# Graph network block on one Trainium2 core: edge rows joined by ScalarE in the first stage, attention logits made by VectorE alone, spare count cells zeroed first

## The reference

```python
# L0: three attention layers, 4 heads of 24
h = x @ W; e = leaky_relu(alpha_s[src] + alpha_d[dst], 0.2)
alpha = softmax of e over the edges of each dst
x = relu(segment_sum(h[src] * alpha, dst) + b)
# L1: sum of neighbours, two dense layers, norm over the nodes
# L2: dot-product attention over the edges, scores clipped to +-10
# L3: messages from edge features
msg = relu(x[src] + edge_attr @ We + be); aggr = segment_sum(msg, dst)
# then two dense layers and a norm over the nodes
```

## Time and profile before

| | us |
|---|---|
| median of 3 runs (5859.54 to 5867.38) | 5861.98 |
| profiled execution | 5863.81 |
| its span | 5862.1 |

### The profile page before, as it was taken

The page is one execution under the profiler, slowest core; times in us unless marked ns, Lnnn a source line. Parts: engine busy times, 40 slices in busy tenths (PEclk is TensorE's granted clock), DMA queues, the critical chain, the costliest instruction groups (busy, mean ns, idle before and its releaser), DMA issues. The chain is left out here.

```text
span 5862.1 us, 68109 instructions
## 1 busy us (share of the span) xinstructions
PE 3511.6 (60%) x25247; PEld 2219.0 (38%) x25248; DVE 3123.5 (53%) x3383; ACT 2625.6 (45%) x4143; POOL 3883.7 (66%) x3309
## 2 busy tenths in 40 slices
PE   3211222221034699988999889997868781667764
PEld 2211111111034455555555555554433330455542
DVE  3644555554369555445555455555579992333323
ACT  1000000000023689888888789894059891222211
POOL 1888888888884577666776578773020787777772
PEclk7555555555566899999999999998989995677765
DMA  8222222222279699757997479875542332332222
GB/s 296 20 18 20 20 18 10 1 1 0 9 251 361 169 195 199 161 115 150 195 193 156 103 164 201 184 153 152 178 166 79 109 130 74 110 81 74 75 53 24
DMA packets 427191, 683.75 MB, mean 117 GB/s; under 512 B 177678, under 2 KB 272397, under 8 KB 422768
## 3 DMA queue, kind: packets, MB, share of 16 engines
q0 software_dynamic: 236096, 287.22, 31.9%
q1 hardware_dynamic: 172432, 350.48, 17.8%
q10 hardware_dynamic: 18336, 41.70, 2.1%
HBM read 540.73 MB, written 138.43 MB: 116 GB/s over the span
## 5 line engine op out<-in xcount | busy, mean ns | idle before, releaser
L330 POOL DMA_INDIRECT counts<-plcell_add,plcell_slot x806 | 1253.9, 1556 | 385.4 <-issue 223.2
L1704 POOL DMA_INDIRECT emxg<-xtab,emsrc x856 | 944.0, 1103 | 448.4 <-issue 257.8
L714 ACT ACT_TABLE_LOAD x1 | 1.3, 1283 | 1613.2 <-PE mtps L702 1613.2
L377 PE MATMUL plpsR<-plpiece,plbefore 128*128 128x500 bf16 (+1 forms) x81 | 47.1, 582 | 813.8 <-DVE plranked L507 800.6
L422 DVE TENSOR_REDUCE plnlow<-plsame 128x13 f32<-128x1664 bf16 x62 | 117.0, 1888 | 661.6 <-DMA counts<-plcell_add,plcell_slot 661.5
L1788 PE MATMUL dotbanks<-emmsg,emsame 128*128 128x96 f32 x1712 | 316.3, 344 | 237.4 <-DVE emsame L1968 230.1
L1176 ACT ACTIVATE ga1prob<-ga1psE,ga1src_fifth 128x512 f32<-128x512 f32 (+1 forms) x700 | 407.2, 680 | 81.8 <-PE ga1psE L1281 79.1
L1176 ACT ACTIVATE ga2prob<-ga2psE,ga2src_fifth 128x512 f32<-128x512 f32 (+1 forms) x700 | 407.5, 683 | 77.0 <-PE ga2psE L1281 74.1
L1176 ACT ACTIVATE ga0prob<-ga0psE,ga0src_fifth 128x512 f32<-128x512 f32 (+1 forms) x700 | 407.1, 678 | 77.7 <-PE ga0psE L1281 74.7
L1788 PEld LDWEIGHTS dotbanks<-emmsg,emsame 128*128 128x128 f32 x1712 | 287.2, 250 | 382.2 <-issue 379.5
L1281 PE MATMUL ga0psE<-ident,ga0logit 128*128 128x128 f32 x2500 | 394.5, 288 | 55.8 <-DMA ga0logit<-log_counts 32.7
(11 more groups left out here) (403 smaller groups left out, 8577.9 us busy)
## 6 DMA issues: line engine op xcount, KB each, us to landing
ga0logit<-log_counts POOLq DMA_DIRECT2D x88, 512.0 KB
ga1logit<-log_counts POOLq DMA_DIRECT2D x88, 512.0 KB
ga2logit<-log_counts POOLq DMA_DIRECT2D x88, 512.0 KB
counts<-plzeros SPq DMA_DIRECT2D x32, 1250.0 KB, 32.7
mthalf<-counts SPq DMA_DIRECT2D x50, 800.0 KB
log_counts<-mtlogs SPq DMA_DIRECT2D x25, 1600.0 KB
ginhalf<-counts SPq DMA_DIRECT2D x50, 800.0 KB
dotlogs<-log_counts ACTq DMA_DIRECT2D x25, 1600.0 KB
```

What stands on the lines that cost most here:

```text
L330: nc.gpsimd.indirect_dma_start(counts[w][:, :], bass.IndirectOffsetOnAxis(ap=cell_slot[:, g % 2, j:j + 1], axis=0), cell_add[:, g % 2, j:j ...
L377: nc.tensor.matmul(psR[:, f // RANK_BANK, 0:k * BINS], before[:], piece[:, n % 2, f:f + k, :].rearrange("p t b -> p (t b)"), start=True, s ...
L714: nc.scalar.activation(logs[:, n % OUTS, q, :], ps[:, u % 3, 0:BW], ACT.Ln, bias=tiny[:, 0:1], scale=math.e).then_inc(log_made, 1)
L1704: nc.gpsimd.indirect_dma_start(xg[:, h, t, :], None, xtab[:, :], bass.IndirectOffsetOnAxis(ap=src[:, g, t:t + 1], axis=0)).then_inc(gather ...
```

## The change

Three things. (1) The spare cells of both tables are zeroed ahead of the bulk, each by one row of 128 cells from one partition. (2) In the first stage, once the sorted list is cleared, SP loads each group's features, ACT joins them with the ends into whole rows (two copies), and SP stores these in DRAM; this is paced by two adds of table 1 per group. The scatter then loads finished rows into three buffers with one DMA per group, and the slots of a stage with one DMA; its copies, its memset and its loads of ends and features are gone. (3) In the layers DVE makes the kept logits alone: a clamp as for the added tiles, then an addition of the loaded mask; ACT's bias instruction is gone, and the mask buffers are freed by DVE's addition. DVE's order in a run becomes: added clamps, kept clamps, kept additions, then the output or the columns. Semaphores are renamed accordingly.

```diff
+WHOLE_BUFS = 3
...
-        edges = {"slot": nc.dram_tensor("edge_slot", [P, ET], i32), "ends": nc.dram_tensor("edge_ends", [P, ET, 2], f32),
+        edges = {"slot": nc.dram_tensor("edge_slot", [P, ET], i32), "rows": nc.dram_tensor("edge_rows", [P, ET, RW], f32),
...
+        feat = sb("feat", [P, WHOLE_BUFS, G, ED])
+        whole = sb("whole", [P, WHOLE_BUFS, G, RW])
...
                 for part, done in zip(counts, zeroed):
+                    sp.dma_start(part[NP * NP:NP * NP + P, :].rearrange("(p f) o -> p (f o)", p=1), zeros[0:1, 0:P]).then_inc(done, 16)
+                for part, done in zip(counts, zeroed):
                     v = part[0:NP * NP, :].rearrange("(p j f) o -> j p (f o)", p=P, f=ZF)
                     for j in range(ZEROS):
                         sp.dma_start(v[j], zeros[:]).then_inc(done, 16)
-                    sp.dma_start(part[NP * NP:NP * NP + P, :], zeros[:, 0:1]).then_inc(done, 16)
...
+                features = a["edge_attr_32"].rearrange("e k -> (e k)")
+                most = features[0:(P - 1) * ET * ED].rearrange("(p f) -> p f", f=ET * ED)
+                rest = features[(P - 1) * ET * ED:E * ED].rearrange("(p f) -> p f", p=1)
+
+                def load_features(g):
+
+                    k = g % WHOLE_BUFS
+                    if g >= WHOLE_BUFS:
+                        sp.wait_ge(whole_made, 2 * (g - WHOLE_BUFS + 1))
+                    flat = feat[:, k, :, :].rearrange("p t k -> p (t k)")
+                    sp.dma_start(flat[0:P - 1, :], most[:, g * G * ED:(g + 1) * G * ED]).then_inc(feat_loaded[k], 16)
+                    n = min(G, EREST - g * G)
+                    if n > 0:
+                        sp.dma_start(flat[P - 1:P, 0:n * ED], rest[:, g * G * ED:(g * G + n) * ED]).then_inc(feat_loaded[k], 16)
+
+                sp.wait_ge(feat_cleared, 1)
+                load_features(0)
+                for g in range(NG):
+                    sp.wait_ge(added[1], 16 * (4 * SORTED_GROUPS + 2 * g + 1))
+                    if g + 1 < NG:
+                        load_features(g + 1)
+                    sp.wait_ge(whole_made, 2 * g + 2)
+                    sp.dma_start(edges["rows"][:, g * G:(g + 1) * G, :], whole[:, g % WHOLE_BUFS, :, :]).then_inc(whole_stored[g % WHOLE_BUFS], 16)
...
-                sp.dma_start(edges["ends"][:, :, :], ends[:]).then_inc(stored, 16)
                 sp.dma_start(edges["slot"][:, :], block_i[:]).then_inc(stored, 16)
-                sp.wait_ge(stored, 64)
+                sp.wait_ge(stored, 48)
+                for k in range(WHOLE_BUFS):
+                    sp.wait_ge(whole_stored[k], 16 * len(range(k, NG, WHOLE_BUFS)))
...
+                nc.vector.memset(feat[:], 0.0).then_inc(feat_cleared, 1)
...
+            @block.scalar
+            def _(act):
+                act.wait_ge(ends_made, 1)
+                for g in range(NG):
+                    k = g % WHOLE_BUFS
+                    uses = range(k, g + 1, WHOLE_BUFS)
+                    act.wait_ge(feat_loaded[k], sum(32 if n * G < EREST else 16 for n in uses))
+                    if g >= WHOLE_BUFS:
+                        act.wait_ge(whole_stored[k], 16 * (g // WHOLE_BUFS))
+                    nc.scalar.activation(whole[:, k, :, 0:ED], feat[:, k, :, :], ACT.Copy).then_inc(whole_made, 1)
+                    nc.scalar.activation(whole[:, k, :, ED:RW], ends[:, g * G:(g + 1) * G, :], ACT.Copy).then_inc(whole_made, 1)
...
-                    step(nc.vector.tensor_copy(ends[:, :, 0], local_i[:]))
+                    nc.vector.tensor_copy(ends[:, :, 0], local_i[:]).then_inc(ends_made, 1)
+                    dve.wait_ge(ends_made, 1)
...
-    STAGES = 2
+def edge_scatter(nc, ctx, edges, tag, first, last):
+
+
+
+    STAGES = 3
     count = last - first
-    LISTS = 4
-    slot = sb("slot", [P, LISTS, G], i32)
-    ends = sb("ends", [P, LISTS, G, 2])
-    feat = sb("feat", [P, STAGES, G, ED])
-    stage = sb("stage", [P, STAGES, G, RW])
-    feat_cleared, staged = (sem(n) for n in ("feat_cleared", "staged"))
-    list_loaded = [sem(f"list_loaded{k}") for k in range(LISTS)]
-    feat_loaded = [sem(f"feat_loaded{k}") for k in range(STAGES)]
-    scattered = [sem(f"scattered{k}") for k in range(STAGES)]
+    slot = ctx.enter_context(nc.sbuf_tensor(tag + "slot", [P, max(count, 1) * G], i32))
+    stage = ctx.enter_context(nc.sbuf_tensor(tag + "stage", [P, STAGES, G, RW], f32))
+    slots_loaded = nc.alloc_semaphore(tag + "slots_loaded")
+    rows_loaded = [nc.alloc_semaphore(f"{tag}rows_loaded{k}") for k in range(STAGES)]
+    scattered = [nc.alloc_semaphore(f"{tag}scattered{k}") for k in range(STAGES)]

     def steps(pool):
-        nc.gpsimd.memset(feat[:], 0.0).then_inc(feat_cleared, 1)
-        pool.wait_ge(feat_cleared, 1)
-        flat = a["edge_attr_32"].rearrange("e k -> (e k)")
-        most = flat[0:(P - 1) * ET * ED].rearrange("(p f) -> p f", f=ET * ED)
-        rest = flat[(P - 1) * ET * ED:E * ED].rearrange("(p f) -> p f", p=1)
-        loads = lambda i: 32 if (first + i) * G < EREST else 16

         def load(i):

-            g, k, m = first + i, i % STAGES, i % LISTS
-            pool.dma_start(slot[:, m, :], edges["slot"][:, g * G:(g + 1) * G]).then_inc(list_loaded[m], 16)
-            pool.dma_start(ends[:, m, :, :], edges["ends"][:, g * G:(g + 1) * G, :]).then_inc(list_loaded[m], 16)
-            rows = feat[:, k, :, :].rearrange("p t k -> p (t k)")
+            k, g = i % STAGES, first + i
             if i >= STAGES:
-                pool.wait_ge(staged, 2 * (i - STAGES + 1))
-            pool.dma_start(rows[0:P - 1, :], most[:, g * G * ED:(g + 1) * G * ED]).then_inc(feat_loaded[k], 16)
-            n = min(G, EREST - g * G)
-            if n > 0:
-                pool.dma_start(rows[P - 1:P, 0:n * ED], rest[:, g * G * ED:(g * G + n) * ED]).then_inc(feat_loaded[k], 16)
-
+                pool.wait_ge(scattered[k], 16 * G * (i // STAGES))
+            pool.dma_start(stage[:, k, :, :], edges["rows"][:, g * G:(g + 1) * G, :]).then_inc(rows_loaded[k], 16)
+
+        pool.dma_start(slot[:], edges["slot"][:, first * G:last * G]).then_inc(slots_loaded, 16)
         load(0)
+        pool.wait_ge(slots_loaded, 16)
         for i in range(count):
-            k, m = i % STAGES, i % LISTS
+            k = i % STAGES
             if i + 1 < count:
                 load(i + 1)
-            pool.wait_ge(feat_loaded[k], sum(loads(n) for n in range(k, i + 1, STAGES)))
-            pool.wait_ge(list_loaded[m], 32 * (i // LISTS + 1))
-            if i >= STAGES:
-                pool.wait_ge(scattered[k], 16 * G * (i // STAGES))
-            nc.gpsimd.tensor_copy(stage[:, k, :, 0:ED], feat[:, k, :, :]).then_inc(staged, 1)
-            nc.gpsimd.tensor_copy(stage[:, k, :, ED:RW], ends[:, m, :, :]).then_inc(staged, 1)
-            pool.wait_ge(staged, 2 * i + 2)
+            pool.wait_ge(rows_loaded[k], 16 * (i // STAGES + 1))
             for t in range(G):
-                nc.gpsimd.indirect_dma_start(edges["sorted"][:, :], bass.IndirectOffsetOnAxis(ap=slot[:, m, t:t + 1], axis=0),
+                nc.gpsimd.indirect_dma_start(edges["sorted"][:, :], bass.IndirectOffsetOnAxis(ap=slot[:, i * G + t:i * G + t + 1], axis=0),
                                              stage[:, k, t, :], None).then_inc(scattered[k], 16)
                 yield i * G + t
...
-        BIAS_AT = (1, 5)
+        MASK_FREE_AT = (3, 5)
...
-                        wait(sp, act_biased, free)
+                        wait(sp, logit_ready, free)
...
-                def finish_logit(r, q):
+                def clamp_kept(r, q):

                     j, c, h = runs[r]
                     first, width = RUN_FIRST[c] * P, RUN_TILES[c] * P
-                    dve.wait_ge(act_biased, act_count[r] + kept_tiles(j).index(q) + 1)
+                    if r >= L_BUFS:
+                        dve.wait_ge(turned, run_end(r - L_BUFS))
+                    nc.vector.tensor_scalar(logit[:, r % L_BUFS, q, 0:width], src_row[:, h, first:first + width], dst_bias[:, j % 2, q, h:h + 1],
+                                            low_bias[:, j % 2, q, h:h + 1], ALU.add, ALU.max).then_inc(kept_clamped, 1)
+
+                def finish_logit(r, q):
+
+                    j, c, h = runs[r]
+                    width = RUN_TILES[c] * P
+                    k, uses = mask_slot(r, q)
+                    dve.wait_ge(kept_clamped, kept_count[r] + kept_tiles(j).index(q) + 1)
+                    dve.wait_ge(mask_loaded[k], 16 * (uses + 1))
                     part = logit[:, r % L_BUFS, q, 0:width]
-                    nc.vector.scalar_tensor_tensor(part, src_row[:, h, first:first + width], least[:, block_first[j] + q, h:h + 1], part, ALU.max, ALU.add).then_inc(logit_ready, 1)
+                    nc.vector.tensor_tensor(part, part, mask[:, k, 0:width], ALU.add).then_inc(logit_ready, 1)
...
+                        clamp_kept(r, q)
+                    for q in kept_tiles(0):
                         finish_logit(r, q)
...
```

(47 more changed lines are left out.)

5 lines of the change are left out of this document (1 added, 4 removed).

## The result

The changed kernel takes 6017.0 us (median of 6 runs, 6009.5 to 6033.8) against 5862.2 for the kernel before (5855.3 to 5867.4): ratio 1.0266, 95% interval 1.0252 to 1.0281. Forecast were 5752 and a range that ended at 5835.

| stage | before | changed | e1_split |
|---|---|---|---|
| first stage | 1647.2 | 1897.2 | 1642.2 |
| its adds, seventh to last start | 1503.0 | 1776.8 | 1521.4 |
| table stage | 278.6 | 275.9 | 275.4 |
| three layers with their setups | 2112.0 | 2010.6 | 2013.9 |
| all behind them | 1824.3 | 1823.9 | 1821.3 |

The account below looks back on a forecast made before the run. Bounds: GpSimd's late-starting row of count adds in the first stage; ScalarE biases and DMA in the layers. First stage -20 (-26 + 6) and three layers -90 from 5863.8 give 5753.8, against the median 5752; range 5675 to 5835.

Parts of the forecast that it names:

- Spare cells first: Start of first stage: both 14 us zeroing tails go, seventh add starts at 111.5 instead of 137.5; 26 us, bounds 20 to 28.
- Edge rows in the first stage: First stage: joining rows there disturbs the count adds by 0.05 us per transfer, 124 transfers, 6 us; bounds 0 and 27.
- The rival of disturbed adds: First stage: the 124 transfers cost the adds 0.22 us each, 27 us instead of 6; total 5775, chance 0.08.
- Table stage: Table stage: 5 of 62 groups are scattered there, covered by VectorE's work; zero change.
- Scattering in the layers: Attention layers: GpSimd is relieved of 59 us per layer, worth nothing by itself, but pays for VectorE making all logits.
- The ScalarE bias: Attention layers: removing 168 biases saves 0.44 us per half run without top sums, 25 and 29 us per layer.
- VectorE makes all logits: Attention layers: VectorE rises to 462 us; 16 us of three-tile and 14 of four-tile gain remain, 30 per layer.
- The floor of 96 us of DMA work: Four-tile blocks in the layers: 96 of 101.2 us are DMA work, leaving 5 open; 3.5 taken per block.
- The point against: Layers: longer VectorE operations slow GpSimd's scatter issue by 0.08 us, 20 us per layer, inside the 59 relieved.
- the 1.81 from which it decides: Layers: mean GpSimd scatter issue, in us, from which GpSimd being locked out decides the time.
- the third rival: Layers: GpSimd locked out by VectorE, scatter issue rising from 1.22 to 2.07 us; +64 per layer, total 6036, chance 0.06.
- the prediction's own signs of being right: Among others: seventh add near 111, adds 1.86 to 1.9 us apart, three-tile halves 2.5 to 2.7, scatter issue under 1.4.

Follow-up runs that it names:

- e1_split: The changed kernel with each first-stage feature load cut in two, 112 and 15 partitions: 5757.2 us, ratio 0.9833 to the kernel before.
- e4_join_only: e1_split with the layers' logits made as before (ScalarE adds biases), GpSimd still scattering finished rows: 5801.6 us, ratio 0.9896 to the kernel before.
- e3_logits_only: The kernel before with only the layers' logits made by VectorE, GpSimd still joining the rows: 5881.2 us, ratio 1.0040.

## Why the prediction was wrong, point by point

1. *Spare cells first*: right in kind and nearly in size. 26 us forecast, 23.7 measured, inside 20 to 28. The bulk of table 1 is late next, as the prediction said, but not in the way it had put it, with the six adds on table 0 through by 110. The fifth add lands only when the bulk is through: in the changed kernel and the seven runs with the spare cells first it starts anywhere from 103.3 to 108.0, and the sixth always at 111.8 to 112.3, while the rate of the zeroing falls to 0 by 111 (changed kernel). The seventh then follows the sixth, at 113.8 where 111.5 was forecast.
2. *Edge rows in the first stage*: **this step failed**. It priced 124 transfers at 0.05 us, at most 0.22 (27 us); the row of adds grew by 273.8. (The 59 small loads of the last partition, which it names, are not in the 124.) The price came from the clears of the sorted rows, 54 transfers of 272 KB, which landed 2.0 us after their issue (median). I took the feature load for a transfer of the same kind, counting it and its bytes, and never asked how its 127 partitions are shared out. The kernel of before had no such load on the SP queue to warn of it (the same 127 partitions were loaded by GpSimd's queue); but it cuts the loads of src and dst at 112 on the SP queue, which was there to be read. The Trainium skill's rule cited above gives 127 packets on one engine, which I could have had before. The rival of disturbed adds had the right place and 27 us for 274. With the load cut, the step is 18.4 us: three times the 6 taken, inside 0 to 27, 17 of it the loads.
3. *Table stage*: zero forecast, 2.7 us gained.
4. *Scattering in the layers*: wrong as put. "It waits already, so this is worth nothing by itself" was argued from GpSimd's idle time; e4_join_only gives it 50 us. GpSimd's waits for clamps do not mean that its masks come in time: PE stood for masks 76 us in the three layers. "It pays for point 6" was right, and e3_logits_only shows how fully: without the relief point 6 loses.
5. *The ScalarE bias*: 0.44 us per half run, to the hundredth in the half runs shown (3.46 to 3.02, 2.92 to 2.48).
6. *VectorE makes all logits*: the additions 1.258 us, where I took 1.16; VectorE 456 us, forecast 462. The sum of 30 per layer met 31.9, 37.2 and 28.9. Its split did not: in layers 0, 1 and 2 the three blocks of three tiles gave 8.8, 14.5 and 6.3 us for 16, but the four of four tiles 20.9, 20.4 and 20.3 for 14. So the sum came out by two errors that cancel, which is luck. The floor of 96 us of DMA work was none: block 4 of layer 1 (counted from 0) takes 89.9.

*The point against*: VectorE's longer row did slow GpSimd, by more than the 20 us that I allowed: scatters 247 x 0.22 = 55 us and masks 132 x 0.19 = 25 us in layer 1. The mean of 1.44 stayed below the 1.81 from which it decides by the prediction, a bound that counts the relief in. This is the third rival's mechanism at a quarter of its price. Slower it came out, but not by that rival. Two of the prediction's own signs of being right failed: the adds came 2.22 us apart, not 1.86 to 1.9, and the scatter issue took 1.40 to 1.44 us, not under 1.4.

*The forecast of 5752 beside e1_split's 5757.* With the load cut the total nearly meets the forecast, but not by its terms: in the profiled executions the first stage gave 5 us for 20, the layers 98 for 90, the table stage 3 and the parts behind the layers another 3 for nothing.

## What to carry to other kernels

Before moving a transfer to another queue, read its outermost size, not only its bytes: 127, 97 or 61 partitions from the SP queue passed packet behind packet, 112, 126 or 128 did not, and the transfers beside them (here the adds) came late by a share of it. A cut that costs one more issue per group was worth 255 us of the row of adds. And idle time of an engine is no proof that relieving it is worthless: where it sits in a chain with others, try the parts apart and together (-50, +19 and -96 us here, in three layers).

## What the runs showed of the hardware that was not expected

- A transfer of 127 partitions of 1664 B from the SP queue passed packet behind packet, as on one DMA engine, in 9.6 us at some 22 GB/s; cut at 112 the same bytes passed in 2.1 us at up to 365 GB/s. The SP queue's next issue behind it took 2.69 us instead of 0.25; behind 61 or 97 such partitions it took 0.26, and why isn't known.
- The load delayed the count adds by 31 to 36 ns for each packet of 77 ns, from 61 packets to 127, and the slack that the adds had did not absorb it.
- 128 two-byte cells spread over 128 partitions kept each table waiting 14 us behind its bulk; as one row of 256 B ahead of it they let the first add start 1.1 us after the time estimated for the bulk's end (62), at 63.1.
- With VectorE making all logits (busy 462 us of 663 instead of 353 of 665), GpSimd's work beside it took longer: its copies of 128x416 from 0.90 to 1.25 us, its issues of scatters from 1.22 to between 1.36 and 1.44, of mask additions from 1.09 to 1.27. Without that part of the change (e4_join_only, layer 1) the issues took 1.23 and 1.08. The single operation on two SBUF tensors got shorter meanwhile (1.34 to 1.26 us), so it is not its length; which of VectorE's operations does it wasn't resolved.
